# Table-driven expert tiles: token rows become the stationary operand, one transpose is added, row buffers are released earlier

## The reference

```python
tokens = hidden_states.reshape(-1, H)                    # 2048 x 256
topk_idx, topk_w = _route(tokens, router_weight, router_bias)   # 4 of 32 experts
gate_vals = jax.nn.silu(jnp.einsum('th,eih->tei', tokens, gate_w))   # I = 128
up_vals = jnp.einsum('th,eih->tei', tokens, up_w)
hidden_vals = gate_vals * up_vals
expert_out = jnp.einsum('tei,ehi->teh', hidden_vals, down_w)
sel = jnp.take_along_axis(expert_out, topk_idx[:, :, None], axis=1)
mixed = (sel * topk_w[:, :, None].astype(sel.dtype)).sum(1)
```

## Time and profile before

| | us |
|---|---|
| median of 3 runs (lowest, highest) | 756.36 (754.49, 757.66) |
| the profiled execution | 758.18 |
| its span | 756.4 |
| the expert tiles and table tiles in it | about 559 to 713 |
| reading back and summing | 714.85 to the end |

### The profile page before, as it was taken

How to read it: one execution, slowest core, us unless ns; L and a number is a source line. 1 busy time by engine, 2 the same in 40 slices (tenths; PEclk the granted TensorE clock), 3 DMA queues, 4 the chain that set the end, 5 groups by cost and what they waited for, 6 DMA issues and landing times. The chain is left out here.

```text
span 756.4 us, 24831 instructions
## 1 busy us (share of the span) xinstructions
PE 624.1 (83%) x8098; PEld 521.3 (69%) x8098; DVE 537.2 (71%) x2069; ACT 539.5 (71%) x1558; POOL 520.1 (69%) x672
## 2 busy tenths in 40 slices
PE   2899999999998368887877878877579999999484
PEld 1678888888887257665765766766568887778263
DVE  3988988888886127688988978677527765555374
ACT  3889999999997169988888978675137765565122
POOL 4758999999989833546778787557406765665574
PEclk9999999999999759979999889699879999999787
DMA  9310000000000022242544444423965454554194
GB/s 297 109 31 2 3 2 4 2 16 22 2 3 3 1 78 70 79 127 65 175 128 146 149 135 133 128 92 130 223 174 140 137 155 144 156 166 120 60 343 166
DMA packets 57276, 77.84 MB, mean 103 GB/s; under 512 B 8504, under 2 KB 46656, under 8 KB 57024
## 3 DMA queue, kind: packets, MB, share of 16 engines
q1 hardware_dynamic: 44624, 54.91, 24.9%
q0 software_dynamic: 7680, 16.87, 6.6%
q10 hardware_dynamic: 4848, 4.47, 1.9%
HBM read 44.52 MB, written 27.49 MB: 95 GB/s over the span
## 5 line engine op out<-in xcount | busy, mean ns | idle before, releaser
L1864 POOL DMA_INDIRECT y_rows<-yo,ix x96 | 94.7, 986 | 76.1 <-DVE ix L1952 41.7
L517 ACT ACTIVATE sc<-sc,mn 128x128 f32<-128x128 f32 x256 | 83.1, 420 | 2.2 <-DVE mn L679 2.2
L1948 DVE TENSOR_SCALAR yo<-bank,hT 128x256 f32<-128x256 f32 x96 | 46.4, 483 | 52.7 <-PE bank L2043 51.9
L1999 PE MATMUL bank<-gT,we_hi 128*128 128x128 f16 x768 | 79.8, 219 | 4.4 <-DVE eh L1962 3.5
L1215 POOL DMA_INDIRECT x_rows<-rows,slot_ix x64 | 64.1, 1001 | 21.7 <-issue 17.3
L1284 ACT ACTIVATE scx<-bank,mnx 128x128 f32<-128x128 f32 x256 | 75.0, 447 | 5.5 <-DVE mnx L1378 5.4
L1186 POOL TENSOR_TENSOR we_lo<-east,we_hi 128x256 f16<-128x256 f32 (+1 forms) x80 | 59.5, 770 | 11.8 <-ACT we_hi L1258 11.6
L1999 PEld LDWEIGHTS bank<-gT,we_hi 128*128 (+1 forms) x768 | 52.3, 97 | 21.3 <-issue 12.7
L1887 ACT ACTIVATE gT<-bank 128x512 f16<-128x512 f16 x96 | 56.5, 592 | 11.1 <-PE bank L2031 11.1
L1892 ACT ACTIVATE eh_hi<-eh 128x128 f16<-128x128 f32 x96 | 29.9, 311 | 48.2 <-DVE eh L1962 48.2
L679 DVE CUSTOM_DVE_ANT_0 sc<-bank,rel 128x128 f32<-128x128 f32 x256 | 57.5, 285 | 0.8 <-issue 0.5
(11 more groups left out here) (298 smaller groups left out, 2422.7 us busy)
## 6 DMA issues: line engine op xcount, KB each, us to landing
hT<-x_rows SPq DMA_DIRECT2D x96, 129.0 KB, 2.5
east<-in_experts SPq DMA_DIRECT2D x32, 384.0 KB, 3.5
rows<-xhl SPq DMA_DIRECT2D x16, 512.0 KB, 4.5
hT<-y_rows SPq DMA_DIRECT2D x16, 512.0 KB, 5.3
x_rows<-padrow SPq DMA_DIRECT2D x21, 129.0 KB, 6.9
wst<-in_wcat SPq DMA_DIRECT2D x8, 256.0 KB, 6.5
cst<-in_ctx_t SPq DMA_DIRECT2D x16, 128.0 KB, 3.4
out<-fin ACTq DMA_DIRECT2D x16, 128.0 KB, 4.3
```

Source lines behind the costliest of these rows:

```text
L517: done = act.activation(sc[:, g, j], sc[:, g, j], ACT.Exp, bias=mn[:, n % 2, g, j:j + 1], scale=-1.0)
L1864: pool.indirect_dma_start(c.y_rows, bass.IndirectOffsetOnAxis(ap=ix[:, n % IX], axis=0), yo[:, n % YO], None, bounds_check=NDEST - 1, oob_ ...
L1948: dve.tensor_scalar(yo[:, n % YO], DN_BANK[n % 2][:, 0:D], xg_word(F32, n % G, 1), None, ALU.mult).then_inc(yo_r, 1)
L1999: done = pe.matmul(o[:, m * width:(m + 1) * width], lhs(x_, k, m), rhs(y_, k, m), start=t == 0, stop=t == 5)
```

## The change

Only table tiles change what they compute; the expert tiles keep their form. For a table tile:

- GU: `gT` is stationary and the weights move, gate and up together, 256 columns: six products for twelve. The result has rows on partitions, not hidden features. For that the gate and up halves lie in one tensor: `we_hi` and `we_lo` are three tensors of [P, 2, 4096] each instead of five.
- DVE's product of silu and up takes the routing weight in as well (one instruction with two multiplications); `yo` becomes a plain copy.
- `eh` must be turned back for DN: PE transposes it in float32 into the unused half of the GT bank, lag 8. `eh_hi` and `eh_lo` are then made from PSUM at lag 9, DN comes at lag 11, `yo` at lag 12 (they were 7, 7, 9 and 10). The bank is shared by two writers and two readers, so ACT's `gT` copy waits for `eh_lo` of the tile 8 back, and `eh_hi` waits for the GT of the tile 8 ahead.
- The row buffer of a table tile is released when `eh` and `ix` are done, not at `yo`.
- NT is 95: the table can't have more than NE + 64 − 1 tiles.

```diff
-NT = NB * TOPK + NE
+NT = NE + NB * TOPK - 1
...
+    L_GT, L_GU, L_SILU, L_TR = 2, 4, 6, 8
+    L_HI, L_DN, L_YO = (7, 9), (9, 11), (10, 12)
...
+    TR_BANK = [b[:, D:D + P] for b in banks[5:8]]
...
-            wait(sp, yo_r, n - G + 1)
+            if by_expert(n - G):
+                sp.wait_ge(yo_r, n - G + 1)
+            elif by_table(n - G):
+                sp.wait_ge(eh_r, n - G + 1)
+                sp.wait_ge(ix_r, n - G + 1)
...
+                if by_table(n - L_TR):
+                    act.wait_ge(ehlo_r, n - L_TR + 1)
...
+                    act.wait_ge(tr_ps, n - NE + 1)
+                    act.wait_ge(gt_ps, min(n + L_TR + 1, NT))
+                    act.activation(eh_hi[:, n % U], TR_BANK[(n + L_TR) % len(TR_BANK)], ACT.Copy).then_inc(ehhi_r, 1)
...
+                    dve.tensor_copy(yo[:, n % YO], DN_BANK[n % 2][:, 0:D]).then_inc(yo_r, 1)
...
+                    dve.scalar_tensor_tensor(eh[:, n % U], GU_BANK[n % len(GU_BANK)][:, EI:2 * EI], xg_word(F32, n % G, 1), eg[:, n % U],
+                                             ALU.mult, ALU.mult).then_inc(eh_r, 1)
...
+                    for x_, y_ in ((0, 0), (1, 0), (0, 1)):
+                        for k in range(KT):
+                            done = pe.matmul(GU_BANK[n % len(GU_BANK)][:, 0:2 * EI].rearrange("p (m w) -> p m w", m=2), gT[:, n % U, x_, k],
+                                             E[y_][k][:, :, bass.ds(e, EI)], start=t == 0, stop=t == 5)
...
+            n = i - L_TR
+            if by_table(n):
+                pe.wait_ge(eh_r, n + 1)
+                pe.transpose(TR_BANK[i % len(TR_BANK)], eh[:, n % U], ident[:]).then_inc(tr_ps, 1)
```

## The result

Faster, by 1.6%: 744.86 us (median of 4 runs, 741.01 to 745.36) against 757.01 for the kernel before on the same chip, a ratio of 0.9835 with a 95% interval of 0.9807 to 0.9863, or 12 us. The profiled execution took 745.36 with a span of 743.6, 12.8 less than the one before. 743.0 was forecast, with 739 to 751 as the range.

The account below looks back on a forecast made before the run. TensorE was taken as the limit, with sequencer address operations showing in table tiles. Tiles at 1.38 us for 1.55 gain TensorE 15.9 us; the deeper lag costs 2.6 back; 13.4 less gives 743.0 us, range 739 to 751.

Parts of the forecast that it names:

- GU: Gate and up products of a table tile: six of 256 columns take 0.66 us; other bound 0.22 us more.
- Transpose: One new float32 transpose of 128 columns on TensorE per table tile: 0.11 us.
- T = 1.38: TensorE's time per table tile: 1.32 us, plus 0.04 for a border and 0.02 for pauses; it was 1.55.
- the ring through VectorE: VectorE's work from yo to eh, then the next tile's GU: 1.26 us per tile, 0.12 under 1.38.
- Register loads: TensorE's loads at tiles 48, 64 and 80: 0.65 us late each, as at tile 32; other end 1.25.
- The iterations: From GU of tile 32 to the last GU: 62 iterations instead of 63, 85.8 us, 52 of them at 1.38.
- The tail: After the last GU, tiles drain at POOL's 1.29 us each; deeper lag costs 2.6 us, last scatter at 699.2.
- A: Table tiles: address operations stay visible, or ACT's and DVE's ring binds at 1.5 to 1.6 us; 753.6 us; chance 0.12.
- B: Table tiles: the shared bank closes a ring of waits, 2.24 us a tile, 790 us; chance 0.07.
- C: TensorE's clock falls to 1.2 GHz as transposes take 0.33 of 1.38 us; 815 us; chance 0.02.
- D: More gain than forecast: table tiles at 1.32 us give 3.3 us more, 739.7 us; chance 0.06.
- E: TensorE's queue in a table tile: the change does less than it says; no size, given nothing.

Follow-up runs that it names:

- e10: The kernel before with TensorE's weight addresses of the table tiles constant (wrong experts, sums differ), all products kept: 738.09 us, one run.
- e9: The changed kernel with its gate and up products split into two halves of 128 columns, twelve products, transpose kept: 758.77 us, 1.0008 of before.
- e6: The changed kernel with the float32 transpose of each table tile done twice: 747.88 us, 0.9874 of before.
- e7: The changed kernel with shorter table-tile lags (transpose 7, eh_hi and eh_lo 8, DN 9, yo 10): 742.13 us, 0.9785 of before.
- e8: The changed kernel with 32 registers a load instead of 16: 747.18 us, 0.9875 of before.
- e1: The kernel before with 95 tiles instead of 96, on the chip with slower scatters: 825.59 us, 0.9969 of before.

## Why the prediction was right, point by point

*What bounds it.* TensorE, and in it the sequencer: shown by e10 (1.29 and 1.22 for 1.55) and e9 (gain gone).

*GU.* Forecast 0.66, measured 0.66. The other bound (0.22 more) was not reached.

*Transpose.* 0.11 forecast and measured; twice in e6.

*T = 1.38.* Measured 1.352. The 0.04 and 0.02 that I added for a border and for pauses were 0.03 in all, and of another kind: it is the ring through VectorE that I had put 0.12 below T. `eh` ends 1.14 after GU's start (630.34 to 631.48), as in the old form, since the copy for `yo` takes 0.42 for 0.48 and gives back what the second multiplication took (0.34 for 0.28). I had 1.26 for this ring as one per tile, which T would clear; but GU starts 0.24 after `eh` ends, not 0.06 (no row had shown 0.06; the expert tiles had 0.15, and alternated for this ring already). So every second tile is late. That T came out near is luck in part: a wrong addition of the right size.

*Register loads.* Forecast 0.65 late each, measured 1.07: this term was too small, by 1.3 us in the sum. The sequencer is not as far ahead in table tiles as it was at tile 32: it comes to the load at 622.1, 0.9 after the start of GU, when the array has 0.4 us left. At tile 32 it came at 599.4, 0.3 after the start of an expert tile's GU and 0.9 ahead of the end of DN. The wait for `eh` is not the difference, since that expert tile's GU (599.13) also began 0.15 after `eh`; what holds the sequencer longer in a table tile is not shown.

*The iterations.* GU(32) to the last GU: 85.8 forecast, 86.8 measured. The 52 full steps took 70.6 without the loads (71.8); loads 3.2 (1.95); the seven before and the three behind 13.1 (12.0), where the two steps without DN took 2.65 for 2.10: GU of tile 38 waited for `eh` (the 0.3 in the waits), and at the end three steps took 3.80 for 3.48. GU(32) itself began 0.6 earlier than in the profile before.

*The tail.* Last GU to last scatter: 11.8 forecast, 11.8 measured. e7 shows it from the other side: 9.2 with the short lags.

*The rivals.* A needed T over 1.5; it was 1.352. B needed T over 1.62; ScalarE does wait for `eh_lo` (13.8 us in 30 times over the stage), but it has the time, and TensorE has no wait for it but one of 0.2. C: the clock stayed at 1.00 with a quarter of TensorE's time in transposes, so the rule of the Trainium skill's page "TensorE: Matmul & The Clock Gate" (section "Part 4: PE-mode transpose"), by which a transpose doesn't count as work for the clock gate, changed nothing here. D was near. E: no.

*Luck.* The last GU came 0.5 us after the forecast, but by errors that cancel: the table steps 1.2 us less, the loads 1.3 more, the iterations at the borders 1.0 more, the start of GU(32) 0.6 less, and this last has nothing to do with the change.

The sum for the profiled execution was 13.4 less, and it was 12.8, of which 12.3 are in the stretch; for the median 13.4, and it was 12.2.

## What to carry to other kernels

Where an operand's address is in a register, each new address is an instruction in TensorE's sequencer that a product of 128 columns was too short to hide here, and one of 256 was not; a tile with half as many, wider products was shorter even with a transpose more. What stands between a wait and the first product is hidden by nothing (0.09 us here). Deeper lags cost nothing in the middle of this pipeline and one step of the engine that drains it (GpSimd, 1.29) each at its end. After such a gain look again at every ring that was just below the old pace, over two tiles as well as over one; steps that alternate are its sign.

## What the runs showed of the hardware

- Twelve float16 products of 128 columns take 0.66 us with constant addresses, 0.96 with eight address operations of 32 to 37 ns among them, and 0.86 in e9. Six of 256 columns with four operations take 0.66.
- GU starts 0.15 us after the end of the VectorE instruction that it waits for with constant addresses, 0.24 with register addresses.
- Loading registers blocks TensorE's sequencer: 0.53 us for 2, 1.31 for 16, 2.34 and 2.46 for 32. In the table tiles 0.17, 1.07 and 2.2 of them showed.
- After an idle time of 2.10 us (e8) TensorE ran on at full speed for some 1.1 us and then about 3 us at 1.2 GHz. After 1.59 (e8) and after 0.95 (the changed kernel) its clock did not fall.
- The kernel before took 755 to 758 us on some chips and 828.5 on another, without a cause that was found. Of the 68 us between the spans of e1 and of the kernel before, 44 are in the stretch from first to last scatter, 23 ahead of it.
